# Six output buffers instead of four, four gather buffers instead of three, and two shared additions issued earlier, in an attention + mixture-of-experts kernel

## The reference, cut to what matters

```python
# x: 4096 rows of 512; 32 experts, 4 of them for each row, 128 slots for each expert
topk_idx, topk_w = _gate(x, gate_w, gate_bias)
buf = zeros((E, CAP, H)).at[flat_e, slot].set(x_rep, mode='drop')      # CAP = 128
h = silu(einsum('ech,ehf->ecf', buf, w1)) * einsum('ech,ehf->ecf', buf, w3)
ob = einsum('ecf,efh->ech', h, w2)
y = where(keep, ob[flat_e, slot], 0)
out = (y.reshape(n, K, H) * topk_w[:, :, None]).sum(1)
shared = silu(x @ shared_gate) * (x @ shared_up) @ shared_down
return out + shared
```

## Time and profile before

| | us |
|---|---|
| median of 3 runs | 1669.8 |
| the profiled execution's own time | 1666.62 |
| its span, first to last instruction | 1664.9 |
| PE busy | 1617.9 |
| POOL busy | 818.8 |
| mean granted PE clock, share of full | 0.99 |

### The profile page before, as it was taken

One profiled execution on the slowest core, in us unless ns is written; L12 is line 12 of the kernel. 1 busy time (PEld: TensorE's weight loads), 2 busy tenths in 40 slices (PEclk: granted clock), 3 DMA queues, 4 the chain that ended last, 5 costly groups with the idle time before them and its releaser, 6 DMA issues. The chain is left out here.

```text
span 1664.9 us, 34808 instructions
## 1 busy us (share of the span) xinstructions
PE 1617.9 (97%) x12194; PEld 1155.4 (69%) x12194; DVE 1213.6 (73%) x3508; ACT 820.1 (49%) x2028; POOL 818.8 (49%) x1136
## 2 busy tenths in 40 slices
PE   8999999999999999999999999999999999899975
PEld 5767677777777777767677777777777777555532
DVE  7887676767677776767676778787877766577764
ACT  6664344435343444444443545454554433577763
POOL 3444544545363645454544554646555356344443
PEclk9999999999999999999999999999999999999988
DMA  8754433334343334333433454545454485599984
GB/s 258 175 142 79 83 83 78 83 74 94 71 96 71 87 68 101 69 80 72 90 76 85 96 103 93 112 90 112 92 115 78 97 291 185 140 277 291 299 248 69
DMA packets 394477, 204.12 MB, mean 123 GB/s; under 512 B 347824, under 2 KB 356016, under 8 KB 394304
## 3 DMA queue, kind: packets, MB, share of 16 engines
q1 hardware_dynamic: 380432, 180.27, 44.5%
q0 software_dynamic: 13312, 20.57, 6.4%
q10 hardware_dynamic: 560, 1.05, 0.2%
HBM read 87.15 MB, written 31.36 MB: 71 GB/s over the span
## 5 line engine op out<-in xcount | busy, mean ns | idle before, releaser
L958 ACT ACTIVATE arena<-arena,neg_max 128x256 f32<-128x256 f32 x512 | 253.7, 496 | 378.6 <-DVE neg_max L1265 378.6
L695 POOL TENSOR_SCALAR arena<-arena,prob_scale 128x256 f16<-128x256 f32 x384 | 183.5, 492 | 451.2 <-DVE prob_scale L1274 449.2
L1616 PE MATMUL ps_query<-xn_both,arena 128*128 128x256 f16 x1024 | 279.5, 273 | 1.4 <-DMA xn_both<-xn_half 1.4
L1617 PE MATMUL ps_query<-xn_both,arena 128*128 128x256 f16 x1024 | 279.4, 273 | 0.0
L1618 PE MATMUL ps_query<-xn_both,arena 128*128 128x256 f16 x1024 | 279.4, 273 | 0.0
L1265 DVE CUSTOM_DVE_ANT_0 arena<-ps_score,mask_add 128x256 f32<-128x256 f32 x512 | 186.5, 421 | 126.2 <-PE ps_score L1618 126.2
L1280 DVE SCALAR_TENSOR_TENSOR arena<-arena,prob_scale 128x256 f16<-128x256 f32 x384 | 233.5, 655 | 7.1 <-POOL arena L695 7.1
L1616 PE MATMUL ps_out<-arena,o_t 128*128 128x512 f16 x512 | 194.1, 379 | 2.1 <-DVE o_t L1285 2.1
L1617 PE MATMUL ps_out<-arena,o_t 128*128 128x512 f16 x512 | 194.0, 379 | 0.0
L1618 PE MATMUL ps_out<-arena,o_t 128*128 128x512 f16 x512 | 194.0, 379 | 0.0
L750 POOL DMA_INDIRECT slot_table<-entry,slot_at x128 | 133.9, 1046 | 48.1 <-issue 33.6
(11 more groups left out here) (320 smaller groups left out, 4064.8 us busy)
## 6 DMA issues: line engine op xcount, KB each, us to landing
arena<-w SPq DMA_DIRECT2D x96, 512.0 KB, 6.8
x_in<-x SPq DMA_DIRECT2D x15, 512.0 KB, 3.6
xn_rows<-xn_half SPq DMA_DIRECT2D x15, 512.0 KB, 3.0
out_rows_dram<-x SPq DMA_DIRECT2D x30, 256.0 KB, 2.3
ctx_in<-ctx_t SPq DMA_DIRECT2D x16, 256.0 KB, 3.0
weight_in<-wq SPq DMA_DIRECT2D x8, 512.0 KB, 5.4
weight_in<-wo SPq DMA_DIRECT2D x8, 512.0 KB, 4.7
arena<-arena SPq DMA_TRANSPOSE x256
```

Of the source, the lines that this page charges most:

```text
L695: pool.tensor_scalar(p_rows[:, c, 0, :], probs[:, c, :], prob_scale[:, c:c + 1], 1.0, ALU.mult, ALU.mult).then_inc(norm_hi, 1)
L958: act.activation(probs[:, c, :], probs[:, c, :], ACT.Exp, bias=neg_max[:, c:c + 1], scale=-1.0, accum_out=prob_sum[:, c:c + 1]).then_inc(e ...
L1616: pe.matmul(dst, a.hi, b.hi, start=start and n == 0, stop=False)
L1617: pe.matmul(dst, a.hi, b.lo, start=False, stop=False)
```

## The change

It gives `expert_y` two more buffers, in the unused second halves of `xn_both`, and `rows_in` a fourth, in `x_in[1]`. A copy into `expert_y` now waits for the additions of expert e - 6, and for experts 4 and 5 for none. POOL gathers six experts ahead instead of five; the gather of expert g waits for the transposes of g - 4 instead of g - 3, so that in loop e POOL waits for the same transposes as before. `add_shared(1)` goes right behind the issue of the table's load, and `add_shared(2)` behind the split of piece 21.

```diff
-        rows_in = [rows.bitcast(F16) for rows in (x_in[0][:, 0, :], x_in[0][:, 1, :], x_in[1][:, 0, :])]
+        rows_in = [rows.bitcast(F16) for rows in (x_in[0][:, 0, :], x_in[0][:, 1, :], x_in[1][:, 0, :], x_in[1][:, 1, :])]
...
         expert_y = [x1[:, t, :] for t in range(TB)] + [
-            xn2_half[:, t, :, :].rearrange("p h d -> p (h d)").bitcast(F32) for t in range(TB)]
+            xn2_half[:, t, :, :].rearrange("p h d -> p (h d)").bitcast(F32) for t in range(TB)] + [
+            both[:, :, :, :].rearrange("p h k t -> p (h k t)")[:, 2 * D:4 * D].bitcast(F32) for both in xn_both]
...
             def gather(e):
-                if e >= 3:
-                    pool.wait_ge(pe_rows, e - 2)
+                if e >= 4:
+                    pool.wait_ge(pe_rows, e - 3)
...
             pool.dma_start(table[:, :, :].rearrange("p e c -> p (e c)"),
                            slot_table.rearrange("(p e) c -> p (e c)", e=E)).then_inc(in_table, 16)
+            add_shared(1)
             late_split(17)
             pool.wait_ge(in_table, 16)
...
-            for e in range(3):
+            for e in range(4):
                 gather(e)
             for k in (20, 21):
                 late_split(k)
-            for e in range(3, 5):
+            add_shared(2)
+            for e in range(4, 6):
                 gather(e)
             for k in (22, 23):
                 late_split(k)
-            add_shared(1)
-            add_shared(2)
...
             for e in range(E + 2):
-                if e + 5 < E:
-                    gather(e + 5)
+                if e + 6 < E:
+                    gather(e + 6)
...
             def scale_y(e):
...
-                if e >= 4:
-                    act.wait_ge(added, adds_done["x", e - 4])
-                else:
+                if e >= 6:
+                    act.wait_ge(added, adds_done["x", e - 6])
+                elif e < 4:
                     act.wait_ge(out_rows, 16 * TB * B)
                     act.wait_ge(out_xn2, 16 * B)
```

More of the change, by code:

```diff
@@ L283, in build @@
         scattered = [signal(f"scattered{n}") for n in range(2)]
-        gathered = [signal(f"gathered{n}") for n in range(3)]
+        gathered = [signal(f"gathered{n}") for n in range(4)]
         in_expert = [signal(f"in_expert{n}") for n in range(AHEAD)]
@@ L755, in gather @@
             def gather(e):
-                if e >= 3:
-                    pool.wait_ge(pe_rows, e - 2)
+                if e >= 4:
+                    pool.wait_ge(pe_rows, e - 3)
                 pool.indirect_dma_start(
-                    rows_in[e % 3], None, xn2_rows, bass.IndirectOffsetOnAxis(ap=table[:, e, 0:1], axis=0),
-                    bounds_check=N + CAP - 1, oob_is_err=True).then_inc(gathered[e % 3], 16)
+                    rows_in[e % 4], None, xn2_rows, bass.IndirectOffsetOnAxis(ap=table[:, e, 0:1], axis=0),
+                    bounds_check=N + CAP - 1, oob_is_err=True).then_inc(gathered[e % 4], 16)
             def add_rows(e):
@@ L768, in add_rows @@
                 pool.indirect_dma_start(
-                    out, bass.IndirectOffsetOnAxis(ap=rows, axis=0), expert_y[e % 4], None,
+                    out, bass.IndirectOffsetOnAxis(ap=rows, axis=0), expert_y[e % 6], None,
                     bounds_check=N + 2 * CAP - 1, oob_is_err=True, compute_op=ALU.add).then_inc(added, 16)
@@ L1010, in scale_y @@
                     act.wait_ge(pe_merged, e // 2 + 1)
-                if e >= 4:
-                    act.wait_ge(added, adds_done["x", e - 4])
-                else:
+                if e >= 6:
+                    act.wait_ge(added, adds_done["x", e - 6])
+                elif e < 4:
                     act.wait_ge(out_rows, 16 * TB * B)
                     act.wait_ge(out_xn2, 16 * B)
-                act.activation(expert_y[e % 4], ps_out[e % 2][:, :], ACT.Copy, scale=1.0 / EY_S).then_inc(scaled_y, 1)
+                act.activation(expert_y[e % 6], ps_out[e % 2][:, :], ACT.Copy, scale=1.0 / EY_S).then_inc(scaled_y, 1)
             act.wait_ge(consts, CONSTS)
@@ L1773, in expert_rows @@
             def expert_rows(e):
-                pe.wait_ge(gathered[e % 3], 16 * (e // 3 + 1))
+                pe.wait_ge(gathered[e % 4], 16 * (e // 4 + 1))
                 if e:
@@ L1778, in expert_rows @@
                     pe.wait_ge(placed, B)
-                rows = rows_in[e % 3].rearrange("c (h p k) -> c h k p", h=2, k=KD)
+                rows = rows_in[e % 4].rearrange("c (h p k) -> c h k p", h=2, k=KD)
                 for n in range(2 * KD):
@@ L1824, in merge @@
                 pe.wait_ge(scaled_y, scaled_at(e + 1))
-                pe.matmul(ps_out[0][:, :], pair_match[e // 2 % 2], expert_y[(e + 1) % 4], start=False, stop=True).then_inc(
+                pe.matmul(ps_out[0][:, :], pair_match[e // 2 % 2], expert_y[(e + 1) % 6], start=False, stop=True).then_inc(
                     pe_merged, 1)
```

## The result

The changed kernel took 1660.88 us (median of 10 runs, 1657.75 to 1667.15), the kernel before beside it 1670.47 (10 runs, 1665.92 to 1673.74). The ratio is 0.9952, with a 95% interval of 0.9939 to 0.9965: 8 us faster, between 6 and 10. The forecast was 1660.6 us and a gain of 9.2. A second measurement, with its own runs of the kernel before, gave 0.9950 (0.9930 to 0.9969).

The account below looks back on a forecast made before the run. The prediction took the chain of additions from expert 7 on to bound the kernel's end; -7.9 + 0.7 - 2.0 = -9.2 us against the median 1669.8 gave 1660.6 us, with 8 in 10 between 1653.0 and 1666.5.

Parts of the forecast that it names:

- The sum: Whole kernel: -7.9 for early additions, +0.7 for the first gather, -2.0 for six buffers, together -9.2 us.
- The likeliest case: Whole kernel: the forecast itself, 1660.6 us with the chain of additions setting the end; chance 0.78.
- PE's second stop: PE at 1592 to 1612, behind ACT's wait for additions 18 and 19: 13.7 us lost, not a gain of the end.
- The first rival: End of the kernel: PE sets it, so both stops pay, 20.9 us gained, giving 1648.9 us; chance 0.08.
- The early additions ... gain 7.9 us: PE's first stop, experts 1 to 2: ACT's wait to copy piece 24 goes entirely; 5.9 us of stop plus 2.05 clock.
- the term's 2.05 for the clock: Twelve matmuls of expert 2 after the first stop: run at the lower clock, 4.65 us instead of 2.6.
- Loss 0.7 us: First gather, queued behind sequence 1's additions: lands at 1406.9, PE wants it at 1406.16; bounds 0 to 5.2 us.
- Six buffers ... gain 2.0 us: Chain of additions from expert 19 to 31: last weights come earlier, landings get faster; bounds 1 us lost to 5 gained.
- From 1502 to the end the chain sets the time: From expert 7's addition (1502.33) on: each pair starts when the one before has landed, no gather between waits for PE.
- What the profile was to show: Signs: piece 24's copy unwaited, up products 7.2 us apart, transposes near 1406.2, additions of 19 and 31 about 7 and 9 earlier.

Follow-up runs that it names:

- Experiments 3: Changed kernel with the four additions of shared sequences 5 and 6 left out, products still computed and copied; ratio 0.9899 to the kernel before.
- 4: Kernel before with the four additions of shared sequences 5 and 6 left out, products still computed and copied; ratio 0.9940 to the kernel before.
- 5: Changed kernel where the additions of experts 24, 26 and 28 also wait until their pair's other expert has landed; ratio 1.0023 to the kernel before.
- the three profiles of the longer way: Kernel before, early additions alone (first run), changed kernel with three gather buffers: experts 1 to 17 took 127.9, 131.2, 130.3 us; ratios 1, 0.9957, 0.9957.
- experiment 7: Changed kernel with sequence 3 added in loop 1 and sequences 4, 5 and 6 together in loop 20; ratio 0.9963 to the kernel before.

## Why the prediction was right, and where it was not

- **The sum** was -9.2 us, measured are -8 (6 to 10). The likeliest case is the one that came, by the mechanism it named: the end is set by the additions, and PE's second stop is worth far less than its 13.7 us. Experiments 3, 4 and 5 show this, the last one with no change of work. That the median came out within 0.3 us of the forecast is luck: the intervals of both measurements are over 4 us wide, and of the 10.7 us between the two profiles 4.0 lie between experts 1 and 17 and 3.0 the other way between 17 and 19, which no term of the sum has. The first rival, both stops in full (1648.9), is refuted: 8 us of 20.9 came.
- **"The early additions ... gain 7.9 us"**: right for the profiled execution, where the addition of expert 1 came 7.5 us earlier, counted from the table. The timed runs of the early additions alone bear the term out, 7.2 and 8.9 us. The three other profiles with the late additions price the stop at 4.4 us only, as the clock fell in them not at all or where it cost nothing. But two of these were among the fastest of their kernel's runs (1663.52 where the median is 1668.52, 1657.44 where it is 1661.29), so they need not be the usual execution. The mean granted clock is 0.9907 over the 16 timed runs of the early additions alone and 0.9895 over the 37 of the kernel before beside them, which is an estimated 2.0 us, the size of the term's 2.05 for the clock. A single trace cannot tell how often the clock falls, and that should have widened the bounds of this term downwards.
- **"Loss 0.7 us" for the first gather behind the additions**: PE waited 0.24 us for it, at 1408.96, and 0.7 in the mean of the ten profiles; the term is right. The gather took 8.5 us to land instead of 6.3, and the two additions ahead of it 9.0 and 11.0. By the Trainium skill ("DMA: Bandwidth & Descriptors", Queues, rings and completion order) each DMA engine takes the descriptors of a queue in order. The trace agrees: the second of these additions landed at 1407.6, the gather at 1408.9. That no trace showed a gather behind an addition in a full stretch was a wrong reading: in the kernel before the gather at 1506.16 stands behind two additions, with the DMA engines at 0.97, and landed in 6.9 us.
- **"Six buffers ... gain 2.0 us" through faster landings**: between expert 19 and 31 the five profiles with six buffers and nothing else changed there show 55.1 to 56.6 us, the three with four buffers 57.2 to 60.0, on average 3.0 us more. The steps moved as forecast: from expert 19 to 21 11.6 us instead of 9.4, from 21 to 23 9.5 instead of 13.2, and the last four 34.0 instead of 34.7. The term and its mechanism are right in the profiles. In time the buffers alone gave 2.7 us once and 8.2 once. What of the larger number is real stays open, and so does why the halves alone add up to more than the whole.
- **"From 1502 to the end the chain sets the time"** is the step that was wrong, without harm to the sum. In most profiles the chain of additions holds the path only from expert 17 on. Between expert 7 and 17 it catches up (its lag, from the start of ACT's copy to that of the addition, falls from 20.0 to 7.0 us in the kernel after), and then its gathers wait for PE. Only the three profiles of the longer way have no such wait. The profile of before is one of them, with the lag at 10.2, so it could not be seen there; experiment 7 rested on this error and paid for it.
- **What the profile was to show** came in the main: the copy of piece 24 without a wait for additions, 7.2 us between the up products, no wait of PE at the merge of experts 22 and 23, the copy of expert 31 ready 10.2 us ahead of its addition, steps from expert 7 to 19 that changed by 0.6 us in sum. The additions of experts 19 and 31 came 6.1 and 8.3 us earlier, where about 7 and 9 were forecast. The first transposes came at 1408.96, outside the 1.5 us around 1406.2; the whole stage began 2.4 us later, and counted from the table's load they moved by 0.4.

## What to carry to other kernels

A wait that a busy engine shows is worth its length only if that engine is on the path behind it; compare when a result is ready with when its consumer starts, at the end of the kernel and not only at the stop. Before a step is taken out of a chain, look where the chain last waits for something else: what is saved before that point is lost at it. Of a cost that holds a fall of the clock, price the stop and the clock apart, since one execution may have both and the next only the first.

## What the runs showed of the hardware that was not expected

- The granted clock of PE after the same short stop differs between executions: full throughout after 3.3 us without a matmul in one, half at once for some 3 us after 3.1 and after 3.6 in two others, and in the fourth, after 3.7 us, full for six matmuls more and then half for nearly 7 us.
- The wait for a group of four accumulating DMAs of 256 KB spreads widely. From the first issue to the next addition it took 11.3 to 16.4 us in loop 8 (11 profiles), 13.4 to 17.1 in loop 20 (9 profiles), and 16.2 and 16.5 when moved to loop 14; six of them in loop 20 took 22.8.
- Two accumulating DMAs ahead of the first gather on the same queue made PE wait 0 to 1.3 us for it in ten profiles.
